# Linear attention with group norm on one core: both query products of a block moved next to its projection, with changes to the opening, the denominators and the end

## What is computed

```python
def conv(x, qkv_w, qkv_b, pos_enc, proj_w, proj_b):      # x is the group-normed input
    qkv = xt @ qkv_w.T + qkv_b                            # xt: (b, 6400, 256)
    q, k, v = jnp.split(qkv, 3, axis=-1)
    q = relu(q); k = relu(k + pos_enc)
    z = 1.0 / (jnp.einsum('bic,bc->bi', q, k.sum(axis=1)) + 1e-06)
    kv = jnp.einsum('bjc,bjd->bcd', k, v)
    out = jnp.einsum('bic,bcd,bi->bid', q, kv, z)
    return out @ proj_w.T + proj_b
return x + conv(group_norm(x, groups=32), ...)
```

## Time and profile before

| what | value |
|---|---|
| median of 3 runs | 2602.06 us (2601.71 to 2605.25) |
| the profiled execution | 2602.08 us, its span 2600.3 us |
| PE busy, share of the span | 2559.8 us (98%) |
| DVE, ACT, POOL busy | 1518.7, 1694.9, 1977.8 us (58, 65, 76%) |
| granted TensorE clock | 0.999 of full |
| DMA queue, share of 16 engines | 73.2% |

### The profile page before, as it was taken

One profiled execution on the slowest core, in us unless ns is written; L12 is line 12 of the kernel. 1 busy time (PEld: TensorE's weight loads), 2 busy tenths in 40 slices (PEclk: granted clock), 3 DMA queues, 4 the chain that ended last, 5 costly groups with the idle time before them and its releaser, 6 DMA issues.

```text
span 2600.3 us, 45137 instructions
## 1 busy us (share of the span) xinstructions
PE 2559.8 (98%) x15978; PEld 2205.1 (85%) x15978; DVE 1518.7 (58%) x2414; ACT 1694.9 (65%) x2698; POOL 1977.8 (76%) x1231
## 2 busy tenths in 40 slices
PE   6999999999999999999999999999999999999998
PEld 5878888888888888888888888888888888888886
DVE  7656565565555555555555565656556555555547
ACT  4766666666676666666667666666666666666654
POOL 5958778787886868877788786877878787786875
PEclk9999999999999999999999999999999999999999
DMA  8557777687777877767778677876767777776668
GB/s 268 193 178 258 261 238 264 231 267 238 265 248 247 271 244 252 269 223 264 253 251 275 230 260 235 264 255 235 261 237 264 242 259 252 243 252 214 217 198 303
DMA packets 324190, 642.17 MB, mean 247 GB/s; under 512 B 25728, under 2 KB 47104, under 8 KB 323968
## 3 DMA queue, kind: packets, MB, share of 16 engines
q1 hardware_dynamic: 323968, 639.28, 73.2%
HBM read 519.25 MB, written 119.93 MB: 246 GB/s over the span
## 4 chain that ended last, share of the span: by engine, by line
PE 93%; DMA 2%; DVE 1%; POOL 1%; issue 1%; ACT 1%; SPq 0%; DVEq 0%; ACTq 0%; POOLq 0%
PE banks L615 21%; PE banks L640 21%; PE banks L676 19%; PE banks L627 14%; PE banks L630 7%; PE banks L604 7%; PE banks L661 3%; DMA y<-xr 1%; DMA q<-in_x 1%; POOL q L1402 1%; PE banks L691 1%; PE banks L698 0%; PE banks L837 0%; ACT xn L1150 0%; DMA xs<-in_x 0%
## 5 line engine op out<-in xcount | busy, mean ns | idle before, releaser
L1386 POOL TENSOR_TENSOR kacc<-kacc,kt 128x512 f32<-128x512 f32 x368 | 476.9, 1296 | 285.5 <-ACT kt L1179 283.2
L1372 POOL TENSOR_TENSOR hl<-xn,hl 128x512 fp32r<-128x512 f32 x382 | 486.5, 1295 | 228.1 <-ACT hl L1162 228.0
L615 PE MATMUL banks<-wqk,hl 128*128 128x256 f32 x4608 | 642.6, 289 | 0.7 <-POOL hl L1372 0.7
L915 DVE TENSOR_TENSOR xt<-banks,xt 128x512 fp32r<-128x512 f32 x400 | 274.8, 687 | 579.9 <-ACT xt L1167 579.9
L640 PE MATMUL banks<-hl,wqk 128*128 128x512 f32 x2304 | 595.7, 394 | 0.5 <-DVE xr L945 0.3
L615 PEld LDWEIGHTS banks<-wqk,hl 128*128 128x128 f32 x4608 | 572.7, 190 | 1.1 <-POOL hl L1372 0.9
L676 PE MATMUL banks<-uhl,mhl 128*128 128x512 f32 (+1 forms) x2316 | 538.8, 382 | 3.1 <-DVE xr L945 2.1
L627 PE MATMUL banks<-kk,xt 128*128 128x512 f32 x1600 | 504.4, 397 | 1.7 <-DVE kk L931 1.7
L676 PEld LDWEIGHTS banks<-uhl,mhl 128*128 128x128 f32 x2316 | 423.6, 188 | 88.0 <-issue 2.5
L640 PEld LDWEIGHTS banks<-hl,wqk 128*128 128x128 f32 x2304 | 408.2, 189 | 69.5 <-issue 1.2
L1172 ACT ACTIVATE kk<-banks 128x512 fp32r<-128x512 f32 x400 | 238.8, 597 | 341.4 <-DVE banks L926 339.2
(11 more groups left out here) (132 smaller groups left out, 2407.5 us busy)
## 6 DMA issues: line engine op xcount, KB each, us to landing
posb<-pos_plus_bk SPq DMA_DIRECT2D x375, 256.0 KB, 4.8
xs<-in_x SPq DMA_DIRECT2D x184, 512.0 KB, 6.9
xa<-in_x SPq DMA_DIRECT2D x184, 512.0 KB, 6.0
xr<-in_x SPq DMA_DIRECT2D x184, 512.0 KB, 3.9
zb<-z_rows SPq DMA_DIRECT2D x184, 512.0 KB, 6.1
y<-xr SPq DMA_DIRECT2D x184, 512.0 KB, 7.3
z_rows<-zt SPq DMA_DIRECT2D x32, 256.0 KB, 3.2
xr<-in_pos SPq DMA_DIRECT2D x25, 256.0 KB, 5.0
```

Source lines behind the costliest of these rows:

```text
L615: last = mm(psK[:, par(n, h), i * C:(i + 1) * C], hl_of(t)[:, a, c, s:s + P], wqk[:, w, c, C:2 * C], start=(j == 0), stop=(j == len(terms) ...
L915: v.tensor_tensor(xt[:, hp, 1, :, :].rearrange("p i n -> p (i n)"), psT, xt[:, hp, 0, :, :].rearrange("p i n -> p (i n)"), ALU.subtract).t ...
L1372: g.tensor_tensor(hl_of(t)[:, 1, :, s], xn_of(n, t)[:, :, s], hl_of(t)[:, 0, :, s], ALU.subtract).then_inc(xl_ready, 1)
L1386: g.tensor_tensor(both, both, kt[:, par(n, h), :], ALU.add).then_inc(ks_done, 1)
```

## The change

1. **PE**: in every step but those of batch 0 before its tail, Qb stands right behind Qa and right ahead of Out, in one run of 6 + 6 + 12 products of 512 columns; behind the gram of the even half nothing is left but the batch's small products. **The banks turn**: Out goes to banks 1 and 2, with m = 1 first into bank 1 and m = 0 second into bank 2, which is Qa's bank. So the second half of Out waits for `save_q` of m = 0 (in the tail's projection both halves do). The denominators go to bank 0.
2. **ACT**: `save_q` of m = 0 stands behind `key_keep` instead of ahead of it; `save_q` of m = 1 stands between `normalise` and `xn_high` of the same step instead of at the step's end.
3. **Denominators**: the 512 columns of a block are taken as two halves f into different rows, so each matmul has 256 columns and there are twice as many; z_plus and the reciprocal work on 256 columns, one reciprocal in step 1 and one in step 3.
4. **Opening**: DVE instead of POOL makes the first low half; 7 idle products instead of 12; in batch 0 the second of two statistics blocks, and its load, stand at the end of the step.
5. **End**: the last image's blocks have a buffer each, and all its loads are issued before its stores; `store_z` of the second group is issued earlier; ACT makes two of the left-over blocks' high parts earlier, the product of the projection weights stays in its PSUM bank, and one high and low part of the last image stand ahead of its high and low parts.

```diff
             def query_a(n, t):
 
                 qn, qt = q_at(n, t)
+                pn, pt = (n, t - 1) if t else (n - 1, LAST)
+                if has_out(pn, pt):
+                    pe.wait_ge(out_ready, two_no(*out_of(pn, pt), CC - 1))
                 wait(pe, q_saved, two_no(qn, qt, 0) - CC)
+                query(qn, qt, 0, 2)
+
+            def query_b(n, t):
+
+                qn, qt = q_at(n, t)
+                wait(pe, q_saved, two_no(qn, qt, 1) - CC)
                 if n > 0 and n < B and t in (1, 3):
                     pe.wait_ge(zt_ready, 2 * (n - 1) + (1 if t == 1 else 2))
-                query(qn, qt, 0, 2)
...
-                def bank_free(m):
-                    if m == 0:
-                        pe.wait_ge(q_saved, two_no(qn, qt, 0) - 1)
+                def bank_free(j):
+                    if j == 1 or ot == LAST:
+                        pe.wait_ge(q_saved, two_no(qn, qt, 0))
...
-                output(on, ot, u, psX[:, 0:2], bank_free)
+                output(on, ot, u, psX[:, 1:3], bank_free, (1, 0), 1)
...
                 if has_q(n, t):
                     query_a(n, t)
+                    if not early(n, t):
+                        query_b(n, t)
                 if has_out(n, t):
                     out_step(n, t, uhl)
...
-                if has_q(n, t):
+                if has_q(n, t) and early(n, t):
                     query_b(n, t)
...
-            keep_running(12)
+            keep_running(7)
...
                 key_high(n, 2 * t)
+                key_keep(n, 2 * t)
                 if has_q(n, t):
                     save_q(*q_at(n, t), 0, 2)
-                key_keep(n, 2 * t)
                 if (n, t) == (B - 1, LAST):
                     return
                 if t < LAST:
                     normalise(n, t + 1)
+                if has_q(n, t):
+                    save_q(*q_at(n, t), 1, 0)
+                if t < LAST:
                     xn_high(n, t + 1)
...
-                if has_q(n, t):
-                    save_q(*q_at(n, t), 1, 0)
...
-                if t in (3, 4) and junction:
-                    invert(n - 1, 1, (t - 3,))
+                if t == 3 and junction:
+                    invert(n - 1, 1)
...
-                for sn, s in stats_at(n, t):
+                for sn, s in stats_at(n, t)[:1 if first(n) else None]:
                     block_stats(sn, s)
```

More of the change, by code:

```diff
@@ L23 @@
 QSLOTS = 13
-WIN = 12
+WIN = 20
 GN_EPS = 1e-5
@@ L331, in has_q, with early @@
             return n > 0 or t >= 2
+        def early(n, t):
+            return first(n) and t < LAST
         def stats_at(n, t):
@@ L513, in step @@
                     next_pos(n, 2 * t + 1)
+                if first(n):
+                    for sn, s in stats_at(n, t)[1:]:
+                        next_xs(sn, s)
                 if has_out(n, t) and (n, t) != (B - 1, LAST):
@@ L649, in denominators, with output @@
                     for c in range(CC):
[L651 to L654, removed]
-                                cols = slice(j * HALF // 4, (j + 1) * HALF // 4)
-                                data = q_of(n, LAST)[:, c, cols]
-                            else:
-                                cols = slice(0, BLK)
-                                data = q_of(n, t)[:, c, :]
-                            last = mm(bank[32 * j:32 * j + 32, cols], swin[:, c, w:w + 32], data,
-                                      start=(s == 0 and c == 0), stop=(s == 1 and c == CC - 1))
+                        for f in range(2):
+                            w = WIN - 16 * s - 2 * c - f
+                            for j in range(4):
+                                t = 8 * g + 4 * s + j
+                                if g == 1 and s == 1:
+                                    if f == 1:
+                                        continue
+                                    k = HALF // 4
+                                    cols, data = slice(0, k), q_of(n, LAST)[:, c, j * k:(j + 1) * k]
+                                else:
+                                    cols, data = slice(0, HALF), q_of(n, t)[:, c, f * HALF:(f + 1) * HALF]
+                                last = mm(bank[32 * j:32 * j + 32, cols], swin[:, c, w:w + 32], data,
+                                          start=(s == 0 and c == 0 and f == 0), stop=(s == 1 and c == CC - 1 and f == 1 - g))
                 last.then_inc(den_done, 1)
-            def output(n, t, u, banks, bank_free):
+            def output(n, t, u, banks, bank_free, order=(0, 1), tail_bank=0):
                 k = size(t)
@@ L990, in step @@
                 key_add(n, 2 * t)
-                if t == 1 and junction:
+                if t == 1 and n > 1:
                     invert(n - 1, 0)
@@ L1018, in step @@
                     key_low(n, 2 * t + 1)
+                if first(n):
+                    for sn, s in stats_at(n, t)[1:]:
+                        block_stats(sn, s)
                 if n + 1 < B:
@@ L1213, in z_plus @@
                 wait(act, z_stored[g], 16 * n)
-                a(zt[:, g, :], bank, ACT.Identity, bias=zeps).then_inc(zt_ready, 1)
+                if g == 1:
+                    wait(act, z_tail_stored, 64 * n)
+                a(zt[:, g, :], bank[:, 0:HALF], ACT.Identity, bias=zeps).then_inc(zt_ready, 1)
             def m_high(n, total):
```

173 lines of the change are left out of this document (87 added, 86 removed).

## The result

| what | before | after |
|---|---|---|
| median of 4 runs each | 2601.89 us (2601.45 to 2605.25) | 2642.36 us (2641.96 to 2645.32) |
| the profiled execution | 2602.08 us, span 2600.3 | 2641.96 us, span 2640.2 |
| PE busy | 2559.8 us (98%) | 2582.7 us (98%) |
| DVE, ACT, POOL busy | 1518.7, 1694.9, 1977.8 us | 1476.3, 1667.4, 1971.2 us |

The changed kernel is **slower**, ratio 1.0156 (95%: 1.0144 to 1.0168), 40.5 us. DVE, ACT and POOL have less to do than before, PE has the same columns (its denominators in twice as many products of half the width), and yet the time is longer: it has gone into waits.

What follows compares the result with a forecast made beforehand. PE was taken as the bound, never waiting between opening and end. From 2602.1 us, plus 49.6 of stalls, less 4.5 for the run, 1.8 for the opening and 3.3 for the end: 2642 us, range 2614 to 2657.

Steps and rivals of the forecast that it cites:

- The stalls: PE waits for late ACT and DVE results in steps 1, 2, 3, 7, 10, 11, 12: 49.6 us more in all.
- steps 7 and 10, Out on the save: With two statistics blocks, Qa's save is released 7.90 us after T against 7.37 due: 0.53 us each.
- The links: Start-to-start times between chained instructions, read from the earlier profile, used to compute when each result reaches PE.
- The run of wide products: Qb moved into PE's wide run takes 1.36 instead of 1.39 us, about 177 steps: 4.5 us saved.
- Rival 3: On PE, the gap goes by width alone, so the run is worth nothing: 2646 to 2647 us; chance 0.10.
- Denominators: On PE, twice as many products of half the width cost the same: 0 taken, up to 4 us in all.
- Opening: First low part from DVE and split statistics shorten PE's early waits: 1.8 us saved (0 to 3.5).
- End: Earlier loads, earlier second store_z and no reciprocal ahead of m_low remove PE's two residual waits: 3.3 us saved.
- the cover holds: Rival: Out's second half and the gram find their results ready in all steps, only gains left: 2592 us; chance 0.12.
- A ring of ACT and DVE: Rival: ACT and DVE's mutual waits lengthen 130 steps by 0.3 us: 39 us more, 2681 us; chance 0.04.
- half as long: Rival: the stalls exist but releases run 0.3 us ahead of the links each: 2617 us; chance 0.12.
- What would show it: Expected signs: PE waits of about 35 us on save_q and 7 on key_low, busy share about 98%, ordinary step 11.98 us.

Runs made afterwards that it cites:

- e6: e5 with both reciprocals behind the even key_low of steps 1 and 3, and step 10's group norm square ahead of u_step; 2593.65 us, ratio 0.9953 to before.
- e1: The changed kernel with ACT's save of m = 0 put back ahead of key_keep; 2604.85 us, ratio 1.0005 to before.
- e5: e1 with the first half of step 11's group norm instructions on ACT moved ahead of the odd x_high_t; 2595.83 us, ratio 0.9972 to before.
- e3: The changed kernel with the old PE order, banks and ACT save places; halved denominators, opening and end as changed; 2596.7 us, ratio 0.9976 to before.
- e7: The kernel before with only the new opening: first low half on DVE, 7 idle products, batch 0 statistics split; 2601.43 us, ratio 0.9997.
- e4: The kernel before with only PE's new order, the turned banks and the saves' new places; old denominators, opening and end; 2681.03 us, ratio 1.0298.
- e2: The changed kernel with DVE's statistics behind key_low instead of ahead of it in the even half; 2613.56 us, ratio 1.0045 to before.

## Why the prediction was right, point by point

The forecast of 2642.0 us fell within 0.4 us of the median. The mechanism was right: PE waits for results that ACT and DVE deliver too late for the new order, in the steps that were named. That the number is so close is luck. The stalls came out 4.4 us larger than forecast and the run's gain 1.0 smaller; against that, opening and end gave 0.8 more each, and 3.9 us went that no term of the sum had (2.0 in batch 1, 1.9 of stalls in the trace of before): +5.4 and -5.5. The range's upper end, 2657, is a little low by its own bounds: 62 us of stalls, nothing from opening and end and 4.5 from the run make 2659.6.

**The stalls**, predicted 49.6 us. Against e6, in which they are gone, the change is 54.0 us longer over batches 1 to 15: 3.8 us in an ordinary batch (predicted 3.62), 4.3 in batch 1 (2.6; it has 0.8 in step 0 and 0.6 in step 2 that I had not counted), 3.15 in batch 14 (3.1), 0.5 in batch 15 (0.5). By place, in an ordinary batch:

| place | predicted | measured | by |
|---|---|---|---|
| steps 7 and 10, Out on the save | 0.53 each | 0.55, 0.34 | e1, starts in step 10 |
| step 11's odd half, gram on key_low | 0.51 | 0.57 | e5 less e1 |
| step 12, Out on the save | 0.74 | 0.67 | e1 |
| step 2, Out of the tail on the save | 0.81 | 0.87 | e1 |
| steps 1 and 3 (the second shows in steps 3 and 4) | 0.5 together | 0.19 + 0.26 | e1, e6 less e5 |
| step 10, group norm's small product | none | 0.24 + 0.09 | e1, e6 less e5 |

The links carried this. In step 7, counted from T at 394.48: `key_add` (DVE L936) at 2.82 for a predicted 2.80, `key_low` 5.80 for 5.79, `key_keep` 6.56 for 6.57, the save 7.06 for 7.07. In step 12 PE's gram starts 5.62 us after T (458.43 less 452.81), exactly the predicted release. Two things were off and nearly cancel. From the save's start to PE's first product I took 0.83 us; it was so in step 2 (338.40 to 339.23), but 0.73 in step 7 (401.54 to 402.27). Against that, products behind a stall are late themselves: from 464.55 to the T at 466.04 the second half of Out takes 1.49 us, where six at 0.227 are 1.36. The one place I had not seen is step 10, where PE waits for the group norm's variance with Qb no longer in between.

**The run of wide products**, predicted 4.5 us. Qa and Qb take 2.75 together, so Qb 1.36, and an ordinary step is 0.03 shorter, both as forecast. But only nine steps of a batch have it (0.02 or 0.03 each), so that it is 0.23 a batch, 3.5 us in all. Batch 1 is a further 2.0 shorter in e6, and the trace of before has two short stalls of its own (1.3 us at the start of batch 14, 0.55 at the end of batch 13) that the other traces do not have there (e3 has two such in batches 4 and 8): 7.4 us together, which is why 54.0 of stalls make only 46.6. What made batch 1 shorter stays open; e3 has it too, e7 has not.

**Rival 3**, that the run is worth nothing, is out: step after step is 0.03 us shorter, and the cheaper place moved with Qb. It is a small effect, 0.25% of a step. The Trainium skill, TensorE: Matmul & The Clock Gate, section Back-to-back issue gap, gives 216 ns for 512 columns as the gap of an isolated product, by its width alone, and about 131 ns for 512 columns in a stream of pairs of weight load and product. These traces, where each product has its weight load, disagree with both: 232 ns for the first six and 227 further on.

**Denominators**, predicted 0: on PE that is right (steps 0 and 2 of e3 are within 0.02 us of before, but for its stalls in batches 4, 8 and 13). Their reciprocals were called off PE's path; e4 shows that in the new order they are on it, for some 30 us. The prediction had them in it without saying so, since it counted the chains of steps 1 and 3 with the halved number.

**Opening**, predicted 1.8: it was 1.75 at the first T and 0.9 in batch 0, together 2.6.

**End**, predicted 3.3, by the removal of PE's waits for residuals. The size was about right and **the step was wrong**. PE still waits at the end: 2.0 + 1.2 + 0.8 us in the rows of waits above, where it was 3.3 and 1.5. From the last T to the last matmul it is 70.98 us before, 70.86 after, and 71 to 73.5 in e1 to e7, old end or new. What became shorter lies behind the last matmul. In the kernel before, the timeline of its last instructions:

```profile
2588.38 4.31 PE L676 MATMUL banks<-hl,hl_tail 128*128 128x512 f32 x24
...
2592.39 1.41 DVE L945 SCALAR_TENSOR_TENSOR xr<-banks,biases,xr 128x512 f32<-128x512 f32 x2 [1.16 <-DMA xr<-in_x]
2593.83 0.37 SPq L368 DMA_DIRECT2D y<-xr  x1
2594.61 0.71 SPq L368 DMA_DIRECT2D y<-xs_tail  x1
```

and in the changed one:

```profile
2632.22 4.09 SPq L368 DMA_DIRECT2D y<-q  x3
2632.24 4.31 PE L684 MATMUL banks<-hl,hl_tail 128*128 128x512 f32 x24
...
2636.66 0.87 DVE L955 SCALAR_TENSOR_TENSOR xs_tail<-banks,biases,xs_tail 128x256 f32<-128x256 f32 x2 [0.75 <-PE banks L684]
2637.56 0.37 SPq L368 DMA_DIRECT2D y<-xs_tail  x1
```

Before, a residual waited for its load of x (DMA, 1.16 us) with PE almost done, so two stores were issued late, one behind the other; the span ends 7.6 us after PE's last product (2600.3 less 2592.69). After, the last residual waits for PE alone, all stores but one are issued before PE ends, and it is 3.6 us. e4 and e7, with the old end, have the longer drain, e1, e2, e3, e5 and e6 the shorter (7.5 us, and 3.9, from the last matmul's start).

Most of the 4.0 us is not the late issue. The last store of the kernel before (KB, us from issue to landing):

```profile
y<-xs_tail SPq DMA_DIRECT2D x1, 256.0 KB, 5.2
```

In the changed kernel the same store takes 2.1 us. It is issued 1.9 us behind PE's last product before (2594.61 less 2592.69) and 1.0 after, which is 0.9 us, and lands 3.1 us sooner. Before, earlier loads and stores were still under way then (a store of 512 KB, `y<-xa`, was issued at 2591.3 and landed at 2597.9), which is the likely reason; it was not tried alone, and neither was any one of the end's edits.

**The other rivals.** That the cover holds (2592 us) is wrong for the change and right for e6 (2593.65): the save was not late by nature, only by its place. A ring of ACT and DVE would have shown in every step, and ordinary steps took 11.99. The stalls were not half as long in any step.

**What would show it.** PE's busy share of the middle is 99.0%, not the 98% named, and the waits named are 17.7 and 4.9 us, not 35 and 7: I had forgotten that a wait is counted only from the modelled end of the product before. Their places were right, but for step 10, whose stall shows in no row of waits: Out there is listed as twelve products without a break, 3.07 us to the next T instead of 2.72.

## What to carry to other kernels

Where an engine is busy without a gap, a reordering that saves it 0.03 us a step is a reordering of everybody's slack: write down for each result it needs when it is due in the new order and what stands ahead of its producer, and check the steps that carry extra work, not the ordinary one. An instruction that frees a buffer for the bound engine belongs ahead of one that waits for a third engine; here the one place was worth some 40 us in 2640. And test parts of a change together as well as apart: halving the reciprocals was worth nothing in the old order from batch 2 on and about 30 us in the new.

## What the runs showed of the hardware that I had not expected

**A place in the run has its price.** In all traces products of 512 columns take 0.232 us in the first six behind narrow ones and 0.227 from there on. Behind a stall they are dear again: in step 12's second half of Out the distances are 0.337 once and then 0.228 to 0.236.

**A stall costs more than its idle time.** The first product starts 0.05 to 0.15 us after the releasing instruction ends, and the next one is late by another 0.1: in step 12 the idle row says 0.38 us, and the step is 0.67 shorter without the stall (e1).

**A DVE instruction that takes 6.6 us more than in other traces**, in the profiled executions of e1, e2 and e6, at 80 to 88 us, and in none of the other six traces. DVE, then PE and POOL in e1:

```profile
80.16 7.89 DVE L1050 TENSOR_SCALAR zt<-zt,biases 128x128 f32<-128x128 f32 x2
```

```profile
88.80 1.09 PE L610 MATMUL banks<-ident,xn 128*128 128x128 f32 x4 [3.55 <-DVE xt L925]
```

```profile
85.76 1.93 POOL L1423 TENSOR_TENSOR posb<-xr,mt 128x512 f32<-128x512 f32 x1
```

and the same DVE instructions in the changed kernel:

```profile
80.19 2.37 DVE L1050 TENSOR_SCALAR zt<-zt,biases 128x128 f32<-128x128 f32 x2
```

Windows of e1, during it and behind it:

```profile
85.00:88.80 3.80, 0.25 (x3) 0.03 (x1) 3.80 (x4) 0.00 (x0) 2.69 (x2) 0.80 0.00 0
88.80:94.00 5.20, 5.20 (x22) 4.91 (x23) 3.65 (x7) 3.89 (x6) 1.62 (x2) 0.50 0.22 20
```

Two instructions that take 2.37 us together take 7.89; it is the first of them, with 7.66 us instead of 1.05. PE, which waits 3.55 us for what follows, then runs 5.2 us at a granted clock of 0.50, the level of 1.2 GHz, its four transposes taking 1.09 us instead of 0.60. The step is 6.14 us longer (5.2 in e2, 6.5 in e6). 3.55 us of it is the wait, and half of the 5.2 us at half clock the rest. It is not the whole core that stands still: POOL works on at its usual speed (1.93 us for an addition that takes 2.05 in the change). The DMA engines move nothing for 3.8 us, but this is no sign of it either, since they also rest from 85 to 87 us in the undisturbed trace of the change (share 0.00). The e6 whose profiled execution took 2595.83 us had runs down to 2587.96, which would fit executions without the long instruction; only a profiled one can show it. What causes it stays open.
